# Low parts on one engine, one down product a chunk later, and routing logits in two matmuls instead of three

## The reference, cut to what matters

```python
x = x + xattn(layernorm(x), ctx, ...)     # self attention, cross attention, a dense MLP
x = x + ffn(layernorm(x), ...)

def geglu(x, w1, w2, w3):
    return gelu(x @ w1, approximate=False) * (x @ w2) @ w3
def ffn(x, w1s, w2s, w3s, W1, W2, W3, Wg):
    shared = geglu(xf, w1s, w2s, w3s)           # every token
    idx = argmax(xf @ Wg, axis=-1)              # 2048 tokens x 8 experts
    for e in range(8):                          # only the tokens with idx == e count
        final = final + where(idx == e, geglu(xf, W1[e], W2[e], W3[e]), 0)
    return shared + final
```

## Time and profile before

| | |
|---|---|
| runs | 1264.76, 1267.38, 1266.42 us |
| profiled execution: its own time | 1266.5 us |
| its span, first to last instruction | 1264.8 us |
| mean granted TensorE clock | 0.996 |
| PE, PEld busy | 97%, 93% |
| DVE, ACT, POOL busy | 79%, 69%, 56% |

### The profile page before, as it was taken

How to read it: one execution, slowest core, us unless ns; L and a number is a source line. 1 busy time by engine, 2 the same in 40 slices (tenths; PEclk the granted TensorE clock), 3 DMA queues, 4 the chain that set the end, 5 groups by cost and what they waited for, 6 DMA issues and landing times.

```text
span 1264.8 us, 31447 instructions
## 1 busy us (share of the span) xinstructions
PE 1225.6 (97%) x10447; PEld 1170.8 (93%) x10447; DVE 993.7 (79%) x2680; ACT 878.3 (69%) x2261; POOL 707.2 (56%) x1104
## 2 busy tenths in 40 slices
PE   7899999999999999999999998999999999999998
PEld 5899999999999999999999997999999999998898
DVE  6898888888899988888888897445455888888864
ACT  5778788888878888888888875444224667777642
POOL 4766656656678756556656678786333223333351
PEclk9999999999999999999999999999999999999999
DMA  6060000000000005000000100010023777777722
GB/s 192 2 242 19 12 8 18 18 2 18 27 2 26 27 2 193 27 2 26 27 2 27 35 2 26 28 49 27 1 97 122 236 246 248 236 238 246 252 93 81
DMA packets 74383, 100.60 MB, mean 80 GB/s; under 512 B 5616, under 2 KB 53616, under 8 KB 74224
## 3 DMA queue, kind: packets, MB, share of 16 engines
q1 hardware_dynamic: 72688, 94.40, 22.6%
q0 software_dynamic: 1536, 4.20, 1.0%
HBM read 84.16 MB, written 14.42 MB: 78 GB/s over the span
## 4 chain that ended last, share of the span: by engine, by line
PE 78%; DVE 11%; ACT 5%; issue 4%; POOL 2%; DMA 0%; DVEq 0%; ACTq 0%; POOLq 0%
PE ps_pj L52 9%; PE ps_pj L54 9%; PE ps_pj L53 9%; PE ps_t L946 8%; PE ps_s L936 8%; PE ps_pv L959 7%; PE ps_aux L52 3%; PE ps_aux L54 3%; PE ps_aux L53 3%; ACT probs L1261 3%; PE ps_s L52 3%; PE ps_s L54 3%; PE ps_s L53 3%; PE ps_pv L52 2%; PE ps_pv L53 2%
## 5 line engine op out<-in xcount | busy, mean ns | idle before, releaser
L664 POOL TENSOR_SCALAR probs<-probs,inv 128x256 f32<-128x256 f32 x512 | 236.9, 483 | 224.5 <-DVE inv L1495 223.8
L1261 ACT ACTIVATE probs<-scores,nb 128x256 f32<-128x256 f32 x512 | 253.6, 497 | 19.5 <-DVE nb L1485 19.0
L1485 DVE CUSTOM_DVE_ANT_0 scores<-ps_s,maskf 128x256 f32<-128x256 f32 x512 | 186.7, 420 | 51.5 <-PE ps_s L936 49.3
L1268 ACT ACTIVATE probs_t_hi<-ps_t 128x512 fp32r<-128x512 f32 x256 | 150.9, 590 | 105.4 <-PE ps_t L946 105.4
L1499 DVE TENSOR_TENSOR probs_t_lo<-ps_t,probs_t_hi 128x512 fp32r<-128x512 f32 x256 | 172.8, 675 | 1.4 <-ACT probs_t_hi L1268 1.3
L946 PE MATMUL ps_t<-ident,probs 128*128 128x128 f32 x1024 | 140.0, 279 | 0.6 <-POOL probs L664 0.6
L959 PE MATMUL ps_pv<-probs_t_lo,v_stack 128*128 128x256 f32 x512 | 130.3, 287 | 0.7 <-issue 0.7
L959 PE MATMUL ps_pv<-probs_t_hi,v_stack 128*128 128x256 f32 x512 | 127.6, 282 | 0.0
L946 PEld LDWEIGHTS ps_t<-ident,probs 128*128 128x128 f32 x1024 | 109.7, 141 | 17.9 <-POOL probs L664 0.9
L52 PE MATMUL ps_pj<-xq_hi,wq_lo 128*128 128x256 f32 x368 | 115.3, 313 | 4.3 <-POOL wk_lo L711 4.2
L683 POOL TENSOR_TENSOR heads_t_lo<-joined,heads_t_hi 128x256 fp32r<-128x256 f32 x128 | 94.9, 741 | 35.1 <-ACT heads_t_hi L1277 34.7
(11 more groups left out here) (284 smaller groups left out, 4553.1 us busy)
## 6 DMA issues: line engine op xcount, KB each, us to landing
raw<-in_L_ffn_W SPq DMA_DIRECT2D x96, 512.0 KB, 5.6
slot_rows<-hin SPq DMA_DIRECT2D x3, 768.0 KB, 5.8
rows<-in_x SPq DMA_DIRECT2D x8, 256.0 KB, 2.7
after_self<-rows SPq DMA_DIRECT2D x8, 256.0 KB, 2.9
rows<-after_self SPq DMA_DIRECT2D x8, 256.0 KB, 2.7
cin<-in_ctx SPq DMA_DIRECT2D x8, 256.0 KB, 3.1
after_cross<-rows SPq DMA_DIRECT2D x8, 256.0 KB, 2.1
stage<-in_L_xattn_fc_w SPq DMA_DIRECT2D x2, 1024.0 KB, 9.2
```

The costliest lines, as they stand in the source:

```text
L664: last = pool.tensor_scalar(PR[:, h, t, :], PR[:, h, t, :], inv[:, h, t:t + 1], 1.0, ALU.mult, ALU.mult)
L1261: last = act.activation(PR[:, h, t, :], SM[:, h, t, :], ACT.Exp, bias=nb[:, h, t:t + 1], scale=-1.0, accum_out=sums[:, h, t:t + 1])
L1268: act.activation(flat(PT[0][:, i % 2, h, :, :]), ps_t[h][:, :], ACT.Copy).then_inc(t_hi, 1)
L1485: last = dve.tensor_tensor_reduce(SM[:, h, t, :], ps_s[h][:, t * S:(t + 1) * S], maskf[:, i // PAIRS % 2, :], -SCALE, -LOWEST, ALU.add, AL ...
```

## The change

Three things are changed.

1. `low_on_pool` and its counts go. DVE makes all 12 low parts of every load. In a 128-token step its order is now: gate 0, pieces 0 and 1, [finish], `lo_single` 0, gate 1, low part of the next x, pieces 2 to 5, `lo_single` 1, pieces 6 to 11. One semaphore `w_lo` replaces two, and SP and PE wait on that one.
2. `down_single(step - 1, 1)` is issued one chunk later: after `up_glu(step, 1)` in a 128-token step, after chunk 1 in a 256-token one. `finish(step - 1)` of a 128-token step moves on DVE from behind gate 0 to behind gate 1 of a 256-token step.
3. The high and low part of the routing weights lie side by side, so that x high takes both in one matmul of 16 columns; x low takes the high part alone (8 columns). `choose` then adds the two halves with one more DVE instruction, and the two counts in the same bank move by 128 columns.

```diff
-def low_on_pool(load, n):
-    return n % 2 == 1 and load >= 1 and ORDER[load - 1] == "S"
...
-            eng.wait_ge(w_lo_dve, LOW_DVE[HALVES * load + half])
-            wait(eng, w_lo_pool, LOW_POOL[HALVES * load + half])
+            eng.wait_ge(w_lo, WPIECES * load + 2 * (half + 1))
...
-            for load in range(SLOTS + 1):
-                for n in range(WPIECES):
-                    if low_on_pool(load, n):
-                        weight_lo(load, n)
...
-                        last = product(pe, ps_l[:, col:col + E], tuple(x[:, c, t * P:(t + 1) * P] for x in XQ[1]),
-                                       tuple(w[:, c * E:(c + 1) * E] for w in WG), n == 0 and t == 0 and c == 0, c == KC - 1)
+                        hi, lo = (x[:, c, t * P:(t + 1) * P] for x in XQ[1])
+                        pe.matmul(ps_l[:, col:col + E], lo, WG[:, c, 0, :], start=n == 0 and t == 0 and c == 0, stop=False,
+                                  skip_group_check=True)
+                        last = pe.matmul(ps_l[:, col:col + 2 * E], hi, WG[:, c, :, :].rearrange("p k e -> p (k e)"), start=False,
+                                         stop=c == KC - 1, skip_group_check=True)
...
                     up_glu(step, 0)
                     up_gate(step, 0)
+                    up_glu(step, 1)
                     if after_single:
                         down_single(step - 1, 1)
-                    up_glu(step, 1)
                     turn_gated(step, 0)
...
-                        if j == 0 and after_single:
+                        if j == 1 and after_single:
                             down_single(step - 1, 1)
...
-                link(dve.tensor_copy(logits[:, :, :].rearrange("p t e -> p (t e)"), ps_l[:, 0:TT * E]))
+                both = ps_l[:, 0:2 * TT * E].rearrange("p (t k e) -> p t k e", k=2, e=E)
+                link(dve.tensor_copy(logits[:, :, :], both[:, :, 0, :]))
+                link(dve.tensor_tensor(logits[:, :, :], both[:, :, 1, :], logits[:, :, :], ALU.add))
...
                     gate(step, 0)
-                    weight_lo(load, 0)
+                    weight_lows(load, (0, 1))
                     if is_single(step - 1):
                         finish(step - 1)
                     lo_single(step, 0)
                     gate(step, 1)
                     lo_of_x(("x", step + 1))
-                    weight_lo(load, 2)
-                    weight_lo(load, 4)
-                    weight_lo(load, 6)
+                    weight_lows(load, (2, 3, 4, 5))
                     lo_single(step, 1)
-                    weight_lo(load, 8)
-                    weight_lo(load, 10)
+                    weight_lows(load, range(6, WPIECES))
                     continue
                 gate(step, 0)
-                if is_single(step - 1):
-                    finish(step - 1)
...
                     gate(step, j)
+                    if j == 1 and is_single(step - 1):
+                        finish(step - 1)
                     if splits:
                         weight_lows(load, (2 * j, 2 * j + 1))
```

More of the change, by code:

```diff
@@ L199 @@
 SLOT_TABLE = slot_table()
-def low_on_pool(load, n):
-    return n % 2 == 1 and load >= 1 and ORDER[load - 1] == "S"
-def low_counts(on_pool):
-    counts, total = [], 0
-    for load in range(SLOTS + 1):
[L210 to L216, removed]
 def transposed_order():
@@ L394, in fused @@
         raw_in = [sem(f"raw_in{h}") for h in range(HALVES)]
-        w_hi, w_lo_dve, w_lo_pool = sem("w_hi"), sem("w_lo_dve"), sem("w_lo_pool")
+        w_hi, w_lo = sem("w_hi"), sem("w_lo")
         tr_done, ranked = sem("tr_done"), sem("ranked")
@@ L515, in load_raw @@
                     if load >= 1:
-                        sp.wait_ge(w_lo_dve, LOW_DVE[HALVES * (load - 1) + half])
-                        sp.sem_inc(sp_gate, 1)
-                        wait(sp, w_lo_pool, LOW_POOL[HALVES * (load - 1) + half])
+                        sp.wait_ge(w_lo, WPIECES * (load - 1) + 2 * (half + 1))
                         sp.sem_inc(sp_gate, 1)
@@ L795, in scatter @@
                                             normed[:, t, :], None).then_inc(scattered, 16)
[L797 to L800, removed]
             def gather():
@@ L1014, in count_chosen @@
                 for k, stationary in enumerate((lower, ones)):
-                    last = pe.matmul(ps_l[:, (k + 1) * TT * E:(k + 2) * TT * E], stationary[:, :], chosen_flat, start=True, stop=True,
+                    last = pe.matmul(ps_l[:, (k + 2) * TT * E:(k + 3) * TT * E], stationary[:, :], chosen_flat, start=True, stop=True,
                                      skip_group_check=True)
@@ L1314, in _ @@
                     act.wait_ge(wg_in, 16)
-                    act.activation(WG[0][:, :], flat(wg_raw[:, :, :]), ACT.Copy).then_inc(wg_split, 1)
+                    act.activation(WG[:, :, 0, :], wg_raw[:, :, :], ACT.Copy).then_inc(wg_split, 1)
             def gelu_dense(e):
@@ L1422, in _ @@
                     act.wait_ge(counted, 1)
-                    act.activation(counts[:, :, :, :].rearrange("p k t e -> p (k t e)"), ps_l[:, TT * E:3 * TT * E], ACT.Copy)\
+                    act.activation(counts[:, :, :, :].rearrange("p k t e -> p (k t e)"), ps_l[:, 2 * TT * E:4 * TT * E], ACT.Copy)\
                         .then_inc(counts_ready, 1)
@@ L1565, in weight_lo @@
                 dve.wait_ge(w_hi, WPIECES * load + n + 1)
-                dve.tensor_tensor(lo, src, hi.bitcast(F32), ALU.subtract).then_inc(w_lo_dve, 1)
+                dve.tensor_tensor(lo, src, hi.bitcast(F32), ALU.subtract).then_inc(w_lo, 1)
             def weight_lows(load, ns):
                 for n in ns:
-                    if not low_on_pool(load, n):
-                        weight_lo(load, n)
+                    weight_lo(load, n)
             def finish(step):
```

6 lines of the change are left out of this document (3 added, 3 removed).

## The result

| | before | after |
|---|---|---|
| median (lowest to highest), 4 runs each | 1266.68 us (1264.76 to 1267.38) | 1251.67 us (1251.33 to 1251.84) |
| profiled execution, its span | 1266.5, 1264.8 us | 1251.33, 1249.5 us |
| POOL busy | 56% | 50% |

The ratio is 0.9884, with an interval of 0.9866 to 0.9901: the kernel after is 1.2% faster. The forecast was 1251.0 us.

What follows compares the result with a forecast made beforehand. DVE's list at the end of S steps, stretched by POOL, was taken as the bound in the slots. Slots 12.4 plus logits 3.15 made 15.5 us off 1266.5: 1251.0 us, range 1248.1 to 1257.

Steps and rivals of the forecast that it cites:

- The bound: End of an S step: DVE's list, stretched by POOL, makes PE wait 1.55 us at the down product.
- The spacing of 0.60: DVE's low parts at S step ends: starts 0.60 us apart without POOL, instead of 1.71 when stretched.
- The rival in which the low parts stay long: Gate 0 of P steps: pieces stay stretched although POOL is silent; 35 us slower, 1301 us; chance 0.04.
- The new wait: Chunk 2 of the P step: PE waits 0.19 us for chunk 0's low part, leaving 1.36 gain per boundary.
- the rival of a wait of 1 us: P step, chunk 2: costlier handoffs make the wait about 1 us at seven boundaries, 1256.7 us; chance 0.10.
- the fourth rival: S step's end: the wait only moves elsewhere and only the logits are gained, 1263.3 us; chance 0.04.
- S to S and the last boundary: S to S transpose comes 1.34 us earlier; slot 15 to the shared step loses its whole wait of 1.54.
- The logits: Dense steps: four fewer weight loads save 0.45 us a batch, first batch lost, 3.15 us in all.
- the rival of the transfers: S steps: late raw halves cost PE 0.5 us in each of eight, 4 us, 1255 us; chance 0.06.
- The tail: After the last slot: finish comes 2.3 us later against its step, gathers and `add_found` shift with it; cost 0.
- the bound of 0.5: Step after the last slot: a gate 0 late by about 1.9 us costs PE at worst 0.5 us.

Runs made afterwards that it cites:

- part 1 alone: Kernel before, with DVE making all low parts in the new order; down product, finish and logits as before: 1256.91 us, ratio 0.9924.
- echo: Kernel after, with POOL subtracting SBUF blocks into an unused area at each of the 54 places where it had made low parts: 1288.62 us, one run.
- part 3 alone: Kernel before, with only the routing weights side by side and the logits in two matmuls: 1263.02 us, ratio 0.9979.
- the other one of the same kernel: Kernel after, unchanged, taken again on another run's chip as the measure for the runs beside it: 1252.23 us, ratio 0.9886.
- Part 2 alone: Kernel before, with only the down product and finish one chunk later; POOL still makes half of the S steps' low parts: 1255.2 us, ratio 0.9912.

## Why the prediction was right, point by point

**The bound.** That DVE's list at the end of an S step, stretched by POOL, held PE up was shown from two sides: taking POOL away (part 1 alone) removes the wait, and an echo of POOL's work brings waits back.

**The spacing of 0.60.** All twelve pieces keep it. At this boundary the kernel after is 1020.72 - 1015.69 = 5.03 us ahead (the first piece behind the low part of x, in each kernel). With that added, `lo_single` 1 starts at 1018.10 + 5.03 = 1023.13, gate 0 at 1027.33, and PE goes on at 1029.94: forecast were 1023.12, 1027.32 and 1029.92. It came out so close because DVE is never idle there and each start was counted from the one before; nothing had to be guessed but what is stretched. The rival in which the low parts stay long falls with it (longest piece of the slots: 0.69).

**The new wait.** Forecast 0.19, measured 0.20, seven times. The wait was real, so the count of DVE's list was right, and the rival of a wait of 1 us is out; and 1.35 a pair against 1.36. With the pairs won, the fourth rival, in which only the logits gain, is out as well.

**S to S and the last boundary.** 1.31 against 1.34, and 1.58 against 1.54. The first comes from part 1 alone, the second from either.

**The logits.** From 799.58 on, seven batches gain 3.08; forecast 3.15. The first batch is lost as foreseen: PE's wait for POOL grows by 0.48, from 1.70 to

```profile
823.54 0.21 PEld L952 LDWEIGHTS ps_t<-ident,stage 128*128 128x128 f32 x2 [2.18 <-POOL stage L653]
```

`choose` with its added instruction costs nothing that the stretches show: part 3 alone is level with before from 923.21 on. The spacing of the trace, 0.113 us, was the right price. The Trainium skill ("TensorE: Matmul & The Clock Gate", Back-to-back issue gap) gives about 81 ns, by which the six batches would have gained 24 x 0.081 = 1.9 us as an estimate; they gained 2.68, and the trace decides.

**The transfers.** The DMA share of a pair rose to 0.77, where I had put 0.80, and raw halves land in 4.6 us (median) after 5.6 before:

```profile
raw<-in_L_ffn_W SPq DMA_DIRECT2D x96, 512.0 KB, 4.6
```

The 5.6 need not be owed to the slots' order: part 3 alone, which has it as before, has 5.1. No wait of PE goes back to one of them; the rival of the transfers is out.

**What was mis-sized.** The tail. The forecast moved the gathers by 2.3 us against the steps that use them and gave that no cost. They moved by 49.8 - 46.7 = 3.1, since PE also gained 1.58 at the last boundary, which DVE's `finish` and the gathers behind its store do not share in full: with `finish` at its old place they still come 1.5 later. The cost was 0.72 in the profiled execution (a wait of 0.69 in step 31), and 0.20 in the other one of the same kernel, so over the bound of 0.5 at its worst. The profile of before showed the warning: an `add_found` that already waited 1.25, a sign that little room was left in front of it.

In sum: forecast 12.4 + 3.15 = 15.5; measured in the span 9.46 + 1.31 + 1.58 + 3.08 - 0.72 = 14.7, and the remaining 0.6 of the 15.3 lies before 799.58 us, where the kernels do not differ and the execution of the kernel after was granted more clock. So what the change did was 0.8 less than forecast, nearly all of it the tail. That the profiled executions differ by 15.3, so close to the forecast, is in part luck: the 0.6 hid most of the tail. The mechanism is borne out by the stretches, not by that match.

**What the first part is worth.** It was not needed for the pairs. Part 2 alone has them 1.8 us shorter; part 1 adds its 1.3 at the S to S boundary, and in the two profiled executions the loss in the tail is 0.7 smaller with it, which the scatter of that stretch (0.20 to 0.72 for the same kernel) nearly covers. Parts 2 and 3 without part 1 were not run. An estimate from the stretches, 3.08 + 11.25 + 1.58 - 1.43 = 14.5 us against 14.7, leaves part 1 nothing that these runs can tell from zero when it is added to the other two. With all lows on DVE and two pieces moved behind the gate, both are had: of the kernels tried, this has the lowest median, 1250.0 us against 1252.23 on the same chip, though their ratios' intervals overlap. Its stretches from 828.72 to 1219.95 sum to 16.84 less than before, the kernel after's to 15.03.

## What to carry to other kernels

When two edits remove the same wait, count it once, and then ask of each what it does to the wait that is next: here the edit that freed VectorE's partner made the next instruction of the list late. An instruction list without gaps can be forecast to a hundredth of a microsecond by adding up starts; so spend the care on what may be stretched, and on chains that pass through DMAs, whose landing times scatter. When a step is shortened, look at the work that does not move with it: it comes closer to the end.

## What the runs showed of the hardware

I had not expected how clean the split between reading and writing is: GpSimd writing 128x512 blocks for 56.9 us left the low parts beside it at 681 to 687 ns, while a subtraction of the same size made them up to 1.81 us. A VectorE instruction of 128x512 with one operand in PSUM stayed at 0.67 to 0.70 us beside either. The stretch costs GpSimd less than VectorE: its subtractions, 1.30 us in the earlier trace rows, took 1.29 to 1.82 in the echo. And a wave of four indirect gathers was waited for 2.0 to 2.1 us in 26 of 39 cases (three waits in each of thirteen traces), but 2.2 to 4.1 us in the other thirteen.
